# Turning both halves of x on VectorE from 32x32 blocks, from batch 3 on

## The reference

```python
# x (8, 256, 1024), coeff (8,), ids (8,), mask (8, 1024, 1024) int32,
# W (1024, 1024), b (1024,), weight (8, 1024, 1024), all float32 but ids and mask
def L0(x, W, b, coeff, mask):
    sign = (2 * mask - 1).astype(x.dtype)
    return einsum('bsi,oi->bso', x, W) + b + einsum('bsi,bio->bso', x, sign) * coeff[:, None, None]

def L1(x, weight, ids):
    return einsum('bsi,boi->bso', x, weight[ids])

x = x + L0(x, W, b, coeff, mask)
x = x + L1(x, weight, ids)
```

## Time and profile before

| | us |
|---|---|
| median of 3 runs | 399.57 |
| lowest, highest | 399.2, 401.47 |
| the profiled execution | 400.16 |
| its span in the profile | 398.4 |

### The profile page before, as it was taken

How to read it: one execution, slowest core, us unless ns; L and a number is a source line. 1 busy time by engine, 2 the same in 40 slices (tenths; PEclk the granted TensorE clock), 3 DMA queues, 4 the chain that set the end, 5 groups by cost and what they waited for, 6 DMA issues and landing times.

```text
span 398.4 us, 7261 instructions
## 1 busy us (share of the span) xinstructions
PE 389.9 (98%) x2538; PEld 356.6 (90%) x2538; DVE 356.3 (89%) x349; ACT 256.9 (64%) x321; POOL 51.6 (13%) x78
## 2 busy tenths in 40 slices
PE   8898999999999999999999999999999999999996
PEld 8898999887899999999999999999999999999885
DVE  0699899989998899999999999999999999998830
ACT  2799776746666677676656685677666775765621
POOL 1022020111110101110020011001020101111200
PEclk9999999999999999999999999999999999999999
DMA  8999876997999999998988976999689995644511
GB/s 225 373 314 314 306 160 158 218 242 228 281 260 227 233 210 239 250 228 230 245 270 233 247 184 216 260 226 258 185 252 235 258 224 188 183 133 133 158 54 53
DMA packets 85031, 88.58 MB, mean 222 GB/s; under 512 B 28930, under 2 KB 69890, under 8 KB 84994
## 3 DMA queue, kind: packets, MB, share of 16 engines
q1 hardware_dynamic: 79152, 79.72, 78.3%
q10 hardware_dynamic: 5842, 8.40, 6.2%
HBM read 79.70 MB, written 8.39 MB: 221 GB/s over the span
## 4 chain that ended last, share of the span: by engine, by line
PE 77%; DVE 11%; ACT 5%; DMA 4%; issue 1%; SPq 1%; POOL 0%; DVEq 0%; POOLq 0%
PE second_ps L424 38%; PE first_ps L393 36%; DVE natural L699 2%; DVE w_lo_left L703 2%; ACT masks L495 2%; DMA natural<-in_L_cond_weight_dram 2%; DMA masks<-in_mask_Bx4096x_ik_dram 2%; PE turn_ps L376 2%; DVE masks L684 2%; ACT WT L490 1%; DVE M_lo L692 1%; DVE x_lo L709 1%; DVE h_lo L692 1%; DVE h_lo L720 1%; PE turn_ps L355 1%
## 5 line engine op out<-in xcount | busy, mean ns | idle before, releaser
L393 PE MATMUL first_ps<-x_lo,M_hi 128*128 128x256 f32 x416 | 118.4, 285 | 0.6 <-DVE M_lo L692 0.6
L393 PE MATMUL first_ps<-x_hi,M_lo 128*128 128x256 f32 x416 | 117.7, 283 | 0.0
L393 PE MATMUL first_ps<-x_hi,M_hi 128*128 128x256 f32 x416 | 117.7, 283 | 0.0
L510 ACT CAST M_hi<-masks 128x1024 fp32r<-128x1024 f32 (+1 forms) x57 | 57.6, 1010 | 76.3 <-DVE masks L684 55.6
L684 DVE SCALAR_TENSOR_TENSOR masks<-masks,coeffs,WT 128x1024 f32<-128x1024 f32 x60 | 77.9, 1304 | 13.6 <-ACT WT L490 13.6
L325 POOL TENSOR_TENSOR natural<-natural,ident 32x128 f32<-32x128 f32 x64 | 44.2, 690 | 291.5 <-DMA natural<-in_L_cond_weight_dram 291.5
L393 PEld LDWEIGHTS first_ps<-x_lo,M_hi 128*128 128x128 f32 x416 | 79.7, 192 | 1.9 <-DVE M_lo L692 0.8
L393 PEld LDWEIGHTS first_ps<-x_hi,M_hi 128*128 128x128 f32 x416 | 79.7, 192 | 0.9
L699 DVE STREAM_TRANSPOSE natural<-natural 128x1024 f32<-128x1024 f32 x64 | 78.8, 1234 | 1.6 <-POOL natural L325 1.6
L393 PEld LDWEIGHTS first_ps<-x_hi,M_lo 128*128 128x128 f32 x416 | 79.7, 192 | 0.0
L692 DVE TENSOR_TENSOR M_lo<-masks,M_hi 128x1024 fp32r<-128x1024 f32 (+1 forms) x57 | 67.0, 1175 | 3.5 <-ACT M_hi L510 3.5
(11 more groups left out here) (80 smaller groups left out, 542.1 us busy)
## 6 DMA issues: line engine op xcount, KB each, us to landing
natural<-in_L_cond_weight_dram SPq DMA_DIRECT2D x256, 128.0 KB, 3.8
masks<-in_mask_Bx4096x_ik_dram SPq DMA_DIRECT2D x60, 512.0 KB, 6.7
out_dram<-out_sb ACTq DMA_DIRECT2D x32, 256.0 KB, 4.1
x_nat<-in_x_dram SPq DMA_DIRECT2D x9, 512.0 KB, 7.1
W_nat<-in_L_cond_W_dram SPq DMA_DIRECT2D x8, 512.0 KB, 7.8
x_nat<-in_x_dram SPq DMA_DIRECT2D x80, 32.0 KB, 3.8
natural<-in_mask_Bx4096x_ik_dram SPq DMA_DIRECT2D x4, 512.0 KB, 8.1
natural<-in_x_dram SPq DMA_DIRECT2D x2, 512.0 KB, 9.4
```

Source lines behind the costliest of these rows:

```text
L393: done = nc.tensor.matmul(acc(b, u), left, right, start=(k == 0 and u % 2 == 0 and j == 0), stop=(k == K - 1 and u % 2 == 1 and j == 2))
L510: done = nc.scalar.copy(part.rearrange("p u (a j) -> p a u j", j=SQ), whole[:, :, u0:u0 + part.shape[1], :])
```

## The change

From batch 3 on half 0 of x is treated as half 1 already is. `load_x_blocks` and `turn_x_blocks` take the half as an argument; SyncE issues the 16 DMAs of half 0 in steps 0, 1 and 2 (four, four, eight) of the batch before in place of one load in step 2; `turn_x` leaves TensorE's loop; VectorE turns half 0 at the end of step 4; ScalarE rounds it at the same place as before, now from `x_nat` in SBUF. Both halves' counts of semaphores are renumbered to fit.

```diff
             def load_x(b, half):
                 if b >= 2:
-                    sp.wait_ge(x_turned, turned_count(b - 1, half) + 1 if b > 2 else 3)
+                    sp.wait_ge(x_turned, 3)
...
-            def load_x_blocks(b, k):
-                if b == BLOCK_X:
-                    sp.wait_ge(x_turned, turned_count(b - 1, 1) + 1)
-                else:
-                    sp.wait_ge(x_done, half_count(b - 1, 1) + 1)
+            def load_x_blocks(b, half, k):
+                sp.wait_ge(x_turned if b == BLOCK_X else x_done, half_count(b - 1, half) + 1)
                 for q in range(GRP):
...
-                if 3 <= i < 7 and b + 1 < B:
-                    load_x_blocks(b + 1, i - 3)
-                if i == 2 and b + 1 < B:
-                    load_x(b + 1, 0)
+                if b + 1 < B:
+                    if i < 3:
+                        load_x_blocks(b + 1, 0, i)
+                    if i == 2:
+                        load_x_blocks(b + 1, 0, 3)
+                    if 3 <= i < 7:
+                        load_x_blocks(b + 1, 1, i - 3)
...
             for n in range(OPEN, CHUNKS):
                 b, i = n // K, n % K
                 first(n)
-                if i == 4 and b + 1 < B:
-                    turn_x(b + 1, 0)
...
             def round_x(b, half):
                 source = turned_x
-                if b >= BLOCK_X and half:
-                    act.wait_ge(first_done, K * b)
-                    act.wait_ge(x_blocks_turned, b - BLOCK_X + 1)
-                    source = x_blocks.rearrange("p (k s) -> p k s", s=S)
+                if b >= BLOCK_X:
+                    act.wait_ge(first_done, K * b - (1 - half) * K // 2)
+                    act.wait_ge(x_blocks_turned, 2 * (b - BLOCK_X) + half + 1)
+                    source = x_blocks(half).rearrange("p (k s) -> p k s", s=S)
...
-            def turn_x_blocks(b):
-                dve.wait_ge(x_loaded[1], DMA * (2 + K // 2 * GRP * (b - BLOCK_X + 1)))
-                nc.vector.transpose(x_blocks, x_blocks).then_inc(x_blocks_turned, 1)
+            def turn_x_blocks(b, half):
+                dve.wait_ge(x_loaded[half], DMA * (2 + K // 2 * GRP * (b - BLOCK_X + 1)))
+                nc.vector.transpose(x_blocks(half), x_blocks(half)).then_inc(x_blocks_turned, 1)
...
                 rest_w(g)
                 if b >= BLOCK_X and i == 1:
-                    turn_x_blocks(b)
+                    turn_x_blocks(b, 1)
+                if i == 4 and b + 1 < B:
+                    turn_x_blocks(b + 1, 0)
```

More of the change, by code:

```diff
@@ L171, in x_arrives, with x_blocks @@
             return natural[:, :ST, half * HALF:(half + 1) * HALF] if b == 1 else x_nat[:, half, :, :]
-        x_blocks = x_nat[:, 1, :, :].rearrange("p s c -> p (s c)")
+        def x_blocks(half):
+            return x_nat[:, half, :, :].rearrange("p s c -> p (s c)")
         def x_part(tile, h, b):
@@ L183, in half_count @@
             return 2 * half + b if b < 2 else 2 * b + half
-        def turned_count(b, half):
-            return half_count(b, half) if b < BLOCK_X else 2 * BLOCK_X + b - BLOCK_X
         turned_x = turn_ps[:, :, :].rearrange("p n (k s) -> p (n k) s", s=S)
@@ L240, in load_unit @@
                                  .rearrange("a (c r) f -> r (a c) f", r=SQ)).then_inc(natural_loaded[g % RING], DMA)
-            def load_x_blocks(b, k):
-                if b == BLOCK_X:
-                    sp.wait_ge(x_turned, turned_count(b - 1, 1) + 1)
-                else:
-                    sp.wait_ge(x_done, half_count(b - 1, 1) + 1)
-                for q in range(GRP):
-                    at = HALF + k * P + q * SQ
-                    sp.dma_start(x_blocks[q * SQ:(q + 1) * SQ, k * S:(k + 1) * S].rearrange("r (g j) -> r g j", j=SQ),
-                                 x[b, :, at:at + SQ].rearrange("(g r) j -> r g j", r=SQ)).then_inc(x_loaded[1], DMA)
+            def load_x_blocks(b, half, k):
+                sp.wait_ge(x_turned if b == BLOCK_X else x_done, half_count(b - 1, half) + 1)
+                for q in range(GRP):
+                    at = half * HALF + k * P + q * SQ
+                    sp.dma_start(x_blocks(half)[q * SQ:(q + 1) * SQ, k * S:(k + 1) * S]
+                                 .rearrange("r (g j) -> r g j", j=SQ),
+                                 x[b, :, at:at + SQ].rearrange("(g r) j -> r g j", r=SQ)
+                                 ).then_inc(x_loaded[half], DMA)
             load_x(0, 0)
@@ L364, in turn_x @@
                 n = half_count(b, half)
-                if b > BLOCK_X:
-                    pe.wait_ge(x_done, half_count(b - 1, 0) + 1)
-                elif b < 2:
+                if b < 2:
                     pe.wait_ge(WT_done, W_BEFORE_X[n])
@@ L528, in round_x @@
                 source = turned_x
-                if b >= BLOCK_X and half:
-                    act.wait_ge(first_done, K * b)
-                    act.wait_ge(x_blocks_turned, b - BLOCK_X + 1)
-                    source = x_blocks.rearrange("p (k s) -> p k s", s=S)
+                if b >= BLOCK_X:
+                    act.wait_ge(first_done, K * b - (1 - half) * K // 2)
+                    act.wait_ge(x_blocks_turned, 2 * (b - BLOCK_X) + half + 1)
+                    source = x_blocks(half).rearrange("p (k s) -> p k s", s=S)
                 else:
-                    act.wait_ge(x_turned, turned_count(b, half) + 1)
+                    act.wait_ge(x_turned, half_count(b, half) + 1)
                 nc.scalar.copy(x_half(x_hi, h_hi, b, half), source).then_inc(x_hi_done, 1)
@@ L706, in rest_x @@
             def rest_x(b, half):
-                source = x_blocks.rearrange("p (k s) -> p k s", s=S) if b >= BLOCK_X and half else turned_x
+                source = x_blocks(half).rearrange("p (k s) -> p k s", s=S) if b >= BLOCK_X else turned_x
                 dve.wait_ge(x_hi_done, half_count(b, half) + 1)
```

## The result

The changed kernel takes 404.09 us in the median of five runs (402.67 to 406.23), the kernel before 399.57 (399.2 to 401.47). The ratio is 1.0109 with a 95% interval of 1.0065 to 1.0153: 4.5 us slower. Forecast were 402.1 us and +0.6%, a loss of 2.5 us, with a range of 399.2 to 406.0. The direction and the mechanism were right; by the medians (a loss of 4.5 and of 3.3 us) it came out 0.8 to 2.0 us larger. The quotient of two medians differs from the ratio given by up to 0.14%. Four executions in a slower state or far off all others (402.86 us in e2_no_turn, 473.23 in e6_round_after_sign, 775.01 in e11_mixed_36, 478.96 in the kernel before) are left out of medians and ratios.

A forecast was written before the change was run, and what follows sets the result against it. TensorE bounds the kernel, with VectorE nearly full and the bound after the change. VectorE's last mark comes 2.72 us late, a 1.94 us loss; with 0.6 for landing, span 398.4 becomes 400.9, median 402.1 us (range 399.2 to 406.0).

The forecast's parts named there:

- TensorE's 4.35 us: TensorE's queue: five groups of eight turning matmuls at 0.87 us removed, won there but given back by waiting.
- VectorE's 1.16 us: VectorE's queue, end of step 4: each added 128x1024 transpose of half 0 takes 1.16 us, five in all.
- the marks: VectorE's M_lo of each next batch's first chunk: 45.75 us apart before, forecast 46.4 to 46.7 after.
- Idle (b): VectorE's wait for ScalarE's rounding before the remainder of half 0: 0.39 us, growing by 0.05 us a batch.
- rival C: VectorE regains its 0.39 us wait for ScalarE's rounding each batch; about even, median 400.0 us; chance 0.18.
- The first blocks: Batch 2: VectorE's first turn of half 0 waits 0.6 us for late-landing blocks; bounds 0 and 4.4.
- The sum: Whole kernel: 1.94 us lost to VectorE plus 0.6 of landing; span 400.9 us, median 402.1 us, +0.6%.
- The collisions: 14 VectorE instructions between first and last mark, about 0.25 us longer beside GpSimd's adds; number kept, 1 us allowed either way.
- idle (a): VectorE's wait for TensorE before each next batch's first M_lo: 0.24 to 0.28 us later, too little for the turn.
- The small DMAs: Loads of half 0 in 128 B pieces: an estimated 1.8 us a batch by the skill's packet cost, supporting late data.
- A, late data: Batch 2: blocks land at 127.2, VectorE waits 4.4 us, none made good; median 405.9 us; chance 0.20.
- B: VectorE holds 44.88 us per batch, so TensorE's whole 4.35 us show; median 395.2 us; chance 0.07.

The follow-up runs named there:

- e2_no_turn: Changed kernel without VectorE's transpose of half 0, all DMAs and waits for them kept; 397.64 us, ratio 0.9942 to the kernel before.
- e6_round_after_sign: Changed kernel with ScalarE rounding half 0 in step 5, behind that step's sign, in place of step 6; 400.48 us, ratio 1.0024 to the kernel before.
- e11_mixed_36: Changed kernel with half 0 by blocks in batches 3 and 6 only, rounded in step 5 behind the sign; 398.91 us, ratio 0.9976.
- e1_turn_beside: Kernel before plus two idle 128x416 transposes on VectorE at the end of step 4 of batches 2 to 6; 401.26 us, ratio 1.0033.
- e4_round_early: Changed kernel with ScalarE rounding half 0 in step 5, ahead of that step's sign, in place of step 6; 403.12 us, ratio 1.008.
- e10_mixed_357: Changed kernel with half 0 by blocks in batches 3, 5 and 7 only, rounded in step 5 behind the sign; 398.65 us, ratio 0.9977.
- e7_rest_on_pool: As e6_round_after_sign, with GpSimd making the remainders of both halves of x from batch 3 on in place of VectorE; 408.45 us, ratio 1.0214.
- e9_no_add: Changed kernel with GpSimd's 64 diagonal adds left out, its waits and signals kept; 398.26 us, ratio 0.9964 to the kernel before.
- e12_before_no_add: Kernel before with the same 64 GpSimd diagonal adds left out; 398.85 us, ratio 0.9981 to the unaltered kernel before.
- e3_one_load: Changed kernel with half 0 loaded by one 512 KB DMA in step 2, VectorE's transpose kept; 401.67 us, ratio 1.0043 to the kernel before.
- e5_after_again: Changed kernel run again unaltered, giving the second trace and second-series time; 402.77 us, ratio 1.0097 to the kernel before.

## Why the prediction was right, and where its size was off

**What bounds the kernel.** Right. That VectorE had only 0.24 to 0.28 us a batch in hand in the later batches, though its share is 89%, decided the sign. The earlier trace rows carried it; e1_turn_beside shows it without any other change.

**TensorE's 4.35 us.** Right as an amount (40 matmuls fewer, x2498 for x2538) and right that it would be given back. e2_no_turn shows that even without the turn only part of it comes through.

**VectorE's 1.16 us.** Right: the turns of halves 1 and 0 stand in the changed kernel's chain with 1.16 us (at 295.73) and 1.15 us (at 312.32), and the marks of the second trace average 46.49 us where 46.64 was forecast. In the first they average 46.81, with five collisions more.

**Idle (b).** The kernel before has 1.76 us of it between first and last mark, and the sum added 0.20; measured are 0.68, 0.42, 0.67 and 0.42, 2.19 in all where that makes 1.96. The 0.44 us a batch (0.39 and 0.05) fit two of the four. That ScalarE's place in its queue keeps it alive was right, against rival C, and e6_round_after_sign shows what moving it is worth: 2.3 us. The price of the SBUF source (1036 ns in place of 1000, where 1046 was taken) was right.

**The first blocks.** The mechanism and the place were right. The size was off in the trace of the result: 1.38 us where 0.6 was taken, inside the bounds of 0 and 4.4. Two of its terms failed, in opposite ways, so that the 0.6 us is near by luck. The last of the eight issues was to begin at 116.3 to 116.5, 117.3 at most with the later opening; it began at 122.04, since the eight took 0.83 us each where 0.45 was taken and the issues ahead of them (four blocks in 3.01 us, the unit in 2.42) were slow too. The landing was taken at 6.9 us and took 3.0. In the second trace the wait is 0. It doesn't follow the opening: 1.38 us where the first M_lo was at 102.02, but 0 in e6_round_after_sign at 101.91 and in e4_round_early at 105.13, 0.71 in e10_mixed_357 at 102.83 and 0.54 in e7_rest_on_pool at 100.30. Why SyncE's issues are slow just there stays open. Later batches never waited, in the changed kernel.

**The sum.** Its two halves were 0.23 us less up to the first mark and 3.55 more between the marks. Measured: 0.82 more and 4.25 more in the first trace, 0.11 less and 2.95 more in the second (185.94 against 182.99). The forecast of 223.51 us from the first M_lo to the mark of 7 (324.14 + 0.6 - 101.23) lies between 223.03 and 225.26. The first trace adds 0.79 of opening. Which of these a run without a profile has can't be told, so that the medians' 0.8 to 2.0 us beyond the forecast are not split up further; that stays open.

**The collisions.** The number was kept at 14 between the first and the last mark; 16 and 11 came, 0.25 us each, and this is most of what the two traces lie above and below the forecast between the marks (+0.70 and -0.60 us). Their cost was in the sum, for it left all of VectorE's need in place. What the working didn't say is that the loss consists of them: without the adds the changed kernel is level with the kernel before (e9_no_add, e12_before_no_add). In the kernel before an unlucky batch eats idle (a); now it makes the run longer. I allowed 1 us either way; the changed kernel's runs go from 401.56 to 406.23, those of the kernel before in the same two series from 399.04 to 401.47. The Trainium skill, GPSIMD Engine Reference, section 1 (Specifications), puts the contention on VectorE instructions with two SBUF inputs; the trace agrees, since those that are long, as L703 in the earlier trace rows, have two, and all of them go with the adds. VectorE's transposes, with one input, take 1.22 to 1.25 us in all traces, also beside an add. That the remainder of half 0 becomes exposed by it cost nothing here: up to the mark of batch 7 all remainders of x in the changed kernel take 1212 to 1226 ns, nine of them. That was luck: the remainder of half 0 took 1.48 us once in the trace of e6_round_after_sign (at 134.49), and one of half 1 took 1.49 in the changed kernel's own, later on.

**The small DMAs.** The Trainium skill's rule on transfers under 512 B (DMA: Bandwidth & Descriptors, section Specifications) would give them a price in every batch; the prediction has an estimate of 1.8 us. By e3_one_load there is none of that size: 222.87 us with the large load, 223.03 with the small ones, from the first M_lo to the mark of batch 7.

**The rivals.** A, late data, happened in part, in batch 2 and in one of two traces. B fell: the marks are not 44.9 us apart in any kernel that turns on VectorE in every batch. C fell: idle (b) did not go by itself.

## What to carry to other kernels

Before work is moved off the engine that bounds the kernel, take the need of the one that gets it from its list between two fixed points of a period, less only the idle time in which it waits for the first one; the page's share hides start and tail. An engine with a quarter of a microsecond in hand per 45 us is a second bound, and what it absorbed by that slack (collisions, late loads) shows in full from then on, as length and as spread. Look then for what lengthens its instructions: here GpSimd's small adds cost 0.7 us while TensorE was the bound and 4.5 us or more once VectorE was. If both engines are that close, moving the work in some of the periods only was the best that was found here, and that was 0.2%, within what can be told from nothing.

## What was not expected of the hardware

- GpSimd's work beside VectorE can lengthen either. The 32x128 add, 0.45 us alone, took 1.45 where it began 0.15 us behind VectorE's sum with two inputs in SBUF (at 211.51 in e7_rest_on_pool, 1.28 us and not lengthened); VectorE's M_lo went from 1.23 to 2.34 us where it began behind GpSimd's 2.38 us subtraction.
- Eight DMA issues of 32 KB in a row, each of pieces of 128 bytes, took 6.61 us in batch 2 (5.84 in the second trace), up to 2.12 us for one, and so held back the mask behind them; the same eight took 4.47 us a batch later.
- The opening of identical code differs by up to 5 us from one execution to another (first M_lo of the loop at 100.30 us in e5_after_again, 105.13 in e4_round_early).
